# One iteration of a pipelined attention-and-feed-forward kernel, laid out anew on VectorE, ScalarE, GpSimd and SyncE

## Chip, cores and metric

The kernel runs on one core of a Trainium2 chip. The metric is device time in microseconds (us) of one execution, as the median of several runs. PE is TensorE (PEld its weight loads), DVE is VectorE, ACT is ScalarE, POOL is GpSimd, and SP is SyncE, which here only issues DMAs.

## What is computed

One transformer layer on x of shape (8, 1024, 512), float32, with 16 heads of 32:

```python
Q, K, V = (split_heads(x @ W.T + b) for W, b in ((Wq, bq), (Wk, bk), (Wv, bv)))
scores = jnp.einsum('bhid,bhjd->bhij', Q, K) / jnp.sqrt(jnp.float32(hd))
scores = jnp.where(causal_mask, -jnp.inf, scores) + decay      # decay = -(i - j)
out = jnp.einsum('bhij,bhjd->bhid', jax.nn.softmax(scores, axis=-1), V)
attn = merge_heads(out) @ Wo.T + bo
...
xh = x @ H                                    # Hadamard, 512 x 512
xq = quantize(xh)                             # 4 bits, one scale a row
ffn = jnp.einsum('bsi,oi->bso', xq, ternary(weight))
...
x = x + layernorm(attn(layernorm(x)))
x = x + layernorm(ffn(layernorm(x)))
```

## The kernel before, in words

Only `fast_path` runs for these inputs (a flag computed on the chip would otherwise start `general_path`). The 8192 rows are worked in 32 steps of 256 rows (two tiles of 128), four steps a batch element. Each of the five engines has a program of its own, written out by hand; the engines meet at semaphores alone, and each executes its own list strictly in the order in which it is written. So the order of the calls in `fast_path` is the schedule.

The main loop is `for s in range(STEPS - 1)`, written once for each engine. Iteration s holds work of several steps at once, with n = s + 1, m = s + 2 and k = s - 1:

- step m, front: statistics of x (`front_stats`, DVE), their columns (`front_columns`, POOL), the normalised x (`front_norm`, ACT) and its split into two f16 halves (`front_high`, ACT; `front_low`, DVE), turned by DMA (`turn_x`, SP);
- step n: query and key products (`qk`, PE, groups 0 to 3), kept as a high half (`qk_high_part`, ACT) and a low half (`qk_low_part`, DVE), copied by 12 DMAs into the operand of the scores (`restack`, SP), squares (`square_of`, POOL) and norms (`keep_norms`, DVE), values (`values`, PE; `keep_v`, ACT; `mix_values`, three DMAs on SP), the scores for the row maxima (`scores`, PE, 0 to 3; `maxima` and `split_max`, DVE);
- step s: `turn_max` (PE) and `keep_max` (ACT), `max_rows` (two DMAs), the keys' products (`keys`, PE, four groups of two halves), `exps` (ACT), `clear_future` (POOL, the causal mask, two instructions a group), `weigh` (PE), the reciprocal (`invert`, ACT, a logarithm and an exponential), `normalise` (DVE, three instructions), and the two halves of the result (`heads_high`, ACT; `heads_low`, POOL);
- step k: the output product (`out_product`, PE, tiles 0 and 1), `y_out` and `y_stats` (DVE), `y_columns` (POOL), the residual (`residual`, DVE), the first two levels of the Hadamard transform (`fold`, `fold_again`, DVE), its split (`x2_high`, ACT; `x2_low`, DVE) and turning (`turn_x2`, SP);
- step k - 1, feed-forward: `transform` (PE), `find_scale` (DVE), `square_sum`, `round_levels`, `level` (ACT), `turn_q` (PE), `keep_q` (ACT), `second` (PE), `scale_out` and `z_stats` (DVE), `z_columns` (POOL), `norm_z` (ACT), `finish_out` (POOL, two additions and the DMA of the output).

PSUM: the score tiles and the head outputs have two banks each, and all other products share four, `ps_job`. `ORDER` gives the twenty products of an iteration to these four in turn, and `claim` makes PE wait until the product that held the bank four places earlier has been read. Three of these waits matter below. `values(n, 1)` takes the bank of the second feed-forward product, so PE waits there for `scale_out(k - 1, 1)` on DVE (L1107). `scores(n, 2)` and `scores(n, 3)` wait for `maxima(n, 0)` and `maxima(n, 1)` (L1010). `qk(n, 0)` of the next iteration waits for `keep_norms` (L1002).

Other waits across engines that the prediction speaks of: `out_product(k, 0)` on PE waits for all four `heads_low(k, .)` on POOL; `weigh(s, 3)` waits for `normalise(s, 1)`; `load_res(k)` on SP waits for `finish_out(k - 2)`; `scores(n, 0)` waits for all twelve DMAs of `restack`; and in the first iterations for `load_rows`, the constant rows of the scores' operand.

Lines of the profile: L1316 is every split product (`qk`, `values`, `out_product`), L996 `qk_low_part`, L658 `qk_high_part`, L1032/1034/1037 `normalise`, L1049 `y_out`, L1065 `residual`, L1071/1072 `fold`, L1080/1081 `fold_again`, L1086 `x2_low`, L1107 `scale_out`, L1010 `maxima`, L1002 `keep_norms`, L1017/1019/1022 `split_max`, L514 `clear_future`, L520 `heads_low`, L535/538 `finish_out`, L691/693 `invert`, L376 `restack`, L318 `load_front`, L1417 `keys`.

## Time and profile before

| | |
|---|---|
| time, median of 3 runs | 1220.31 us (1218.34 to 1220.6) |
| the profiled execution | 1217.23 us, span 1215.2 us |
| PE | busy 1106.2 us (91%) |
| DVE | busy 972.1 us (80%) |
| ACT | busy 745.7 us (61%) |
| POOL | busy 661.7 us (54%) |
| DMA queues | 54.7% and 4.7% of 16 engines' span |
| TensorE clock granted | 0.973 in the mean, 1.00 in the middle |
| chain that ended last | DVE 48%, ACT 19%, issue 17%, PE 10% |

Busy time is the union of the instructions' spans on an engine. Matmuls overlap one another in the pipeline, so a busy PE is not the same as a PE that streams all the time; start to start tells that better. "Issue" in the chain is time in which an engine waited for nothing that the profile shows. The first 33 us or so are weights and first products, and from about 1120 us on the last step drains; in between the loop runs with a period of some 35 us.

### The profile page before, as it was taken

Reading aid. Unit: us, or ns where it says so; the run is one execution under the profiler, and the core shown is the slowest. Engines: PE = TensorE matmul, PEld = TensorE weight load, DVE = VectorE, ACT = ScalarE, POOL = GpSimd, SP = SyncE. Lnnn points to the kernel's source line nnn. Section 1 sums busy time; section 2 is a strip of 40 time slices with the busy share of each in tenths; the row PEclk is TensorE's granted clock in tenths of the full one; section 3 lists DMA queues with packets and bytes.
Section 4 is the critical chain, followed back from the end, with each engine's and each line's share of the span. In section 5 each row is a group of like instructions: output and inputs, shape, how many; then the busy total and the mean of one; then the engine's idle time right before and its main releaser. Section 6 shows DMA issues by size and latency. Waiting matters only on the chain.

```text
span 1215.2 us, 45316 instructions
## 1 busy us (share of the span) xinstructions
PE 1106.2 (91%) x18656; PEld 727.5 (60%) x18656; DVE 972.1 (80%) x2082; ACT 745.7 (61%) x1622; POOL 661.7 (54%) x1101
## 2 busy tenths in 40 slices
PE   5899999999999999999999999999999999999551
PEld 3566656666666666666666666666666666666320
DVE  6658998888888888889888888888888889887662
ACT  5445567666566666655667666666766655666441
POOL 2334565565555556555555566565556565565442
PEclk9999999999999999999999999999999999999865
DMA  9746665675667566566665666666666655654231
GB/s 271 175 106 134 120 134 138 151 145 136 128 127 146 134 137 158 129 136 140 126 133 136 155 143 134 128 126 136 146 140 150 136 133 138 130 114 104 69 70 37
DMA packets 204692, 161.85 MB, mean 133 GB/s; under 512 B 150432, under 2 KB 150688, under 8 KB 204384
## 3 DMA queue, kind: packets, MB, share of 16 engines
q1 hardware_dynamic: 199600, 141.34, 54.7%
q0 software_dynamic: 4880, 17.57, 4.7%
q8 instruction: 148, 2.42, 0.9%
q14 instruction: 64, 0.52, 0.2%
HBM read 40.87 MB, written 16.78 MB: 47 GB/s over the span
## 4 chain that ended last, share of the span: by engine, by line
DVE 48%; ACT 19%; issue 17%; PE 10%; DMA 1%; SPq 1%; POOL 1%; POOLq 0%; ACTq 0%; DVEq 0%
PE f_job L1316 7%; DVE f_rmax L1010 5%; DVE f_inverse L1034 4%; DVE f_x2l L1086 4%; DVE f_o L1032 4%; ACT f_stage L658 4%; ACT f_PT L680 3%; DVE f_z L1107 3%; DVE f_y L1072 3%; DVE f_stage L996 3%; ACT f_unread L709 3%; DVE f_fst L968 3%; DVE f_bst L1042 2%; DVE f_o L1037 2%; DVE f_folded_x L1081 2%
## 5 line engine op out<-in xcount | busy, mean ns | idle before, releaser
L514 POOL TENSOR_SCALAR_AFFINE_SELECT f_PT<-f_PT 64x512 f32<-64x512 f32 (+1 forms) x256 | 186.2, 746 | 89.4 <-ACT f_PT L680 58.2
L529 POOL TENSOR_TENSOR f_square<-f_stage 128x512 bf16<-128x512 f16 x128 | 130.3, 1038 | 137.1 <-ACT f_stage L658 125.1
L996 DVE SCALAR_TENSOR_TENSOR f_stage<-f_job,f_bias,f_stage 128x256 f16<-128x256 f32 x256 | 111.2, 476 | 71.8 <-ACT f_stage L658 71.7
L1316 PE MATMUL f_job<-f_xTh,f_wqh 128*128 128x256 f16 x512 | 140.9, 275 | 15.6 <-DVE f_wkl L869 14.3
L698 ACT ACTIVATE f_OTh<-f_o 128x256 f16<-128x256 f32 x128 | 52.2, 408 | 158.4 <-DVE f_o L1037 158.4
L1316 PE MATMUL f_job<-f_xTh,f_wql 128*128 128x256 f16 x512 | 140.1, 274 | 0.0
L1316 PE MATMUL f_job<-f_xTl,f_wqh 128*128 128x256 f16 x512 | 140.1, 274 | 0.0
L1316 PE MATMUL f_job<-f_xTh,f_wkh 128*128 128x256 f16 x512 | 139.7, 273 | 0.0
L1316 PE MATMUL f_job<-f_xTh,f_wkl 128*128 128x256 f16 x512 | 139.7, 273 | 0.0
L1316 PE MATMUL f_job<-f_xTl,f_wkh 128*128 128x256 f16 x512 | 139.6, 273 | 0.0
L1316 PE MATMUL f_job<-f_wvh,f_xTh 128*128 128x512 f16 x256 | 97.8, 382 | 28.7 <-DVE f_z L1107 28.7
L658 ACT ACTIVATE f_stage<-f_job,f_bias 128x256 f16<-128x256 f32 x256 | 105.7, 464 | 20.8 <-PE f_job L1316 14.1
L520 POOL TENSOR_TENSOR f_OTl<-f_o,f_OTh 128x256 f16<-128x256 f32 x128 | 85.1, 665 | 59.7 <-ACT f_OTh L698 59.7
L680 ACT ACTIVATE f_PT<-f_st 128x512 f32<-128x512 f32 x192 | 105.7, 590 | 6.9 <-PE f_st L1417 6.9
L1417 PEld LDWEIGHTS f_st<-f_stacks 128*64 128x64 f16 x2432 | 68.1, 110 | 52.4 <-issue 32.4
L1316 PE MATMUL f_job<-f_woh,f_OTh 128*128 128x512 f16 x256 | 98.6, 385 | 0.4 <-POOL f_OTl L520 0.4
L666 ACT ACTIVATE f_V<-f_job 128x512 f32<-128x512 f32 x64 | 38.1, 597 | 98.9 <-PE f_job L1316 98.9
L1316 PE MATMUL f_job<-f_woh,f_OTl 128*128 128x512 f16 x256 | 97.9, 382 | 0.0
L1316 PE MATMUL f_job<-f_wol,f_OTh 128*128 128x512 f16 x256 | 97.7, 382 | 0.0
L1316 PE MATMUL f_job<-f_wvh,f_xTl 128*128 128x512 f16 x256 | 97.5, 381 | 0.0
L1316 PE MATMUL f_job<-f_wvl,f_xTh 128*128 128x512 f16 x256 | 97.3, 380 | 0.0
L1417 PE MATMUL f_st<-f_stacks 128*64 128x128 f16 (+1 forms) x2432 | 91.8, 214 | 3.9 <-ACT f_PT L684 3.9
(189 smaller groups left out, 3049.8 us busy)
## 6 DMA issues: line engine op xcount, KB each, us to landing
f_stacks<-f_stage SPq DMA_DIRECT2D x380, 128.0 KB
f_xin<-x SPq DMA_DIRECT2D x32, 512.0 KB, 4.6
f_x<-x SPq DMA_DIRECT2D x32, 512.0 KB, 3.9
out<-f_z POOLq DMA_DIRECT2D x32, 512.0 KB, 4.2
f_Vmix<-f_V SPq DMA_DIRECT2D x32, 256.0 KB
f_Vmix<-f_V SPq DMA_DIRECT2D x64, 128.0 KB
f_stacks<-rows_const SPq DMA_DIRECT2D x3, 512.0 KB, 7.1
f_stacks<-wqT SPq DMA_DIRECT2D x2, 512.0 KB, 5.0
```

The source lines that it names most:

```text
L514: nc.gpsimd.affine_select(out=d, in_=d, compare_op=ALU.is_ge, fill=0.0, base=odd * SUB, pattern=[[0, 4], [0, TP], [1, SUB]], channel_multi ...
L520: nc.gpsimd.tensor_tensor(OT[s % 2][1][:, g, :], o32[:, g % 2, :], OT[s % 2][0][:, g, :], ALU.subtract).then_inc(OTl_made, 1)
L529: nc.gpsimd.tensor_tensor(square[:, 2 * m + pair, :], h, h, ALU.mult).then_inc(squared, 1)
L658: nc.scalar.activation(stage[:, 2 * m, g, :], bank("qk", g)[:, m * W2:(m + 1) * W2], ACT.Identity, bias=bias[:, m, g:g + 1]).then_inc(qk_h ...
L680: nc.scalar.activation(dst, src, ACT.Exp, scale=1.0 / SS).then_inc(expd, 1)
L698: nc.scalar.activation(OT[s % 2][0][:, g, :], o32[:, g % 2, :], ACT.Copy).then_inc(OTh_made, 1)
L996: nc.vector.scalar_tensor_tensor(stage[:, 2 * m + 1, g, :], bank("qk", g)[:, m * W2:(m + 1) * W2], bias[:, m, g:g + 1], stage[:, 2 * m, g, ...
L1010: nc.vector.tensor_reduce(rmax[:, n % 2, SLOTS * i:SLOTS * i + SLOTS], score_bank(n, i)[:, 0:SLOTS * BW].rearrange("q (i k) -> q i k", k=B ...
L1032: nc.vector.tensor_tensor(heads, heads, inverse[:, g % 2, :], ALU.mult).then_inc(o_scaled, 1)
L1034: nc.vector.tensor_tensor(inverse[:, g % 2, :], ps_o[g % 2][:, W2:D], inverse[:, g % 2, :], ALU.mult).then_inc(o_error, 1)
L1316: mm = pe.matmul(dst, lhs[a](c), rhs[b](c), start=(n == 0), stop=(n == 3 * KC - 1))
L1417: mm = pe.matmul(ps_st[half][upper * SUB:(upper + 1) * SUB, i * W2 + q * SUB:i * W2 + (q + w) * SUB], Ks[js % 3][:, h, c * SUB:(c + 1) * SUB],
```

## The change

In the loops of DVE, ACT, POOL and SP, calls stand in another order, and some have moved to the next or the previous iteration. PE's program and every operation are as they were. Written out in the difference below; in short:

- SP: `mix_values` of a step is issued one iteration later, after `load_front` and before `restack`; `load_rows` comes after `restack`.
- POOL: `heads_low(k, 3)` stands first, `square_of(n, 1)` after two `clear_future`; `front_columns` works a step ahead and stands between `heads_low(s, 1)` and `heads_low(s, 2)`; `finish_out` is last, behind `heads_low(s, 2)`.
- ACT: `invert(s, 2)`, `heads_high(s, 1)` and `heads_high(s, 2)` have moved into the next iteration, behind `qk_high_part(n, 0)`; `keep_max` stands ahead of `qk_high_part(n, 1)`, both `front_norm` earlier, `level(k - 1, 0)` between the two first `exps`.
- DVE: `front_stats` works a step ahead and stands at the end; both `qk_low_part(n, 2)` and `(n, 3)` stand ahead of `find_scale(k - 1, 1)`; `front_low` ahead of both `y_out`; `scale_out(k - 1, 0)` ahead of `residual`; `scale_out(k - 1, 1)` ahead of `fold_again(k, 1)`; `maxima` are spread out; `normalise(s, 1)` is between the last two.

```diff
@@ -425,19 +425,21 @@
                     load_res(k)
                 if has(m + 1):
                     load_front(m + 1)
-                if s < 2:
-                    load_rows(n)
+                if s:
+                    mix_values(s)
                 restack(n, 0)
                 restack(n, 1)
                 restack(n, 2)
+                if s < 2:
+                    load_rows(n)
                 if has(m):
                     turn_x(m)
-                mix_values(n)
                 if has(k):
                     turn_x2(k, 0)
                     turn_x2(k, 1)
 
             last = STEPS - 1
+            mix_values(last)
             max_rows(last)
             load_res(last - 1)
             turn_x2(last - 1, 0)
@@ -544,18 +546,17 @@
             pool.wait_ge(qk_low, 8)
             for r in range(4):
                 pool.dma_start(*stack_piece(0, 2, r)).then_inc(first_stacked, 16)
+            front_columns(2)
             for s in range(STEPS - 1):
                 n, m, k = s + 1, s + 2, s - 1
-                square_of(n, 0)
                 if has(k):
                     heads_low(k, 3)
-                if has(m):
-                    front_columns(m)
-                if has(n):
-                    square_of(n, 1)
+                square_of(n, 0)
                 if has(s):
                     clear_future(s, 0)
                     clear_future(s, 1)
+                if has(n):
+                    square_of(n, 1)
                 if has(k):
                     y_columns(k)
                 if has(s):
@@ -566,10 +567,12 @@
                     clear_future(s, 3)
                     heads_low(s, 0)
                     heads_low(s, 1)
+                if has(m + 1):
+                    front_columns(m + 1)
+                if has(s):
+                    heads_low(s, 2)
                 if has(k - 1):
                     finish_out(k - 1)
-                if has(s):
-                    heads_low(s, 2)
 
             last = STEPS - 1
             heads_low(last - 1, 3)
@@ -756,41 +759,48 @@
             for s in range(STEPS - 1):
                 n, m, k = s + 1, s + 2, s - 1
                 qk_high_part(n, 0)
+                if s:
+                    invert(k, 2)
                 if has(k):
                     invert(k, 3)
+                if s:
+                    heads_high(k, 1)
+                    heads_high(k, 2)
+                keep_max(s)
                 qk_high_part(n, 1)
-                keep_max(s)
+                if has(m):
+                    front_norm(m, 0)
+                qk_high_part(n, 2)
                 if has(k):
                     heads_high(k, 3)
-                qk_high_part(n, 2)
                 if has(k - 1):
                     square_sum(k - 1, 0)
                     round_levels(k - 1, 0)
+                qk_high_part(n, 3)
                 if has(m):
-                    front_norm(m, 0)
-                qk_high_part(n, 3)
+                    front_norm(m, 1)
+                exps(s, 0, 0)
+                if s == 0:
+                    keep_ffscale()
                 if has(k - 1):
                     level(k - 1, 0)
-                exps(s, 0, 0)
                 exps(s, 0, 1)
-                if s == 0:
-                    keep_ffscale()
-                    keep_tern()
                 if has(m):
-                    front_norm(m, 1)
                     front_high(m)
                 exps(s, 1, 0)
                 exps(s, 1, 1)
+                if s == 0:
+                    keep_tern()
                 if has(k - 1):
                     square_sum(k - 1, 1)
                     round_levels(k - 1, 1)
                     level(k - 1, 1)
                     keep_q(k - 1, 0)
                 invert(s, 0)
-                exps(s, 2, 0)
                 invert(s, 1)
                 if has(k - 1):
                     keep_q(k - 1, 1)
+                exps(s, 2, 0)
                 exps(s, 2, 1)
                 keep_v(n, 0)
                 if has(k):
@@ -802,11 +812,11 @@
                 keep_v(n, 1)
                 if has(k - 1):
                     norm_z(k - 1)
-                invert(s, 2)
-                heads_high(s, 1)
-                heads_high(s, 2)
 
             last = STEPS - 1
+            invert(last - 1, 2)
+            heads_high(last - 1, 1)
+            heads_high(last - 1, 2)
             keep_max(last)
             invert(last - 1, 3)
             heads_high(last - 1, 3)
@@ -1140,56 +1150,56 @@
             maxima(0, 2)
             maxima(0, 3)
             split_max(0)
+            front_stats(2)
             for s in range(STEPS - 1):
                 n, m, k = s + 1, s + 2, s - 1
                 qk_low_part(n, 0)
                 if has(k):
                     normalise(k, 3)
                 qk_low_part(n, 1)
-                if s == 0:
-                    keep_norms(0)
-                if has(m):
-                    front_stats(m)
                 if has(k - 1):
                     find_scale(k - 1, 0)
                 qk_low_part(n, 2)
+                if s == 0:
+                    keep_norms(0)
+                qk_low_part(n, 3)
+                if s < 4:
+                    weight_guard(s)
                 if has(k - 1):
                     find_scale(k - 1, 1)
-                qk_low_part(n, 3)
                 if s == 0:
                     fold_bias()
-                if has(k):
-                    y_out(k, 0)
-                if s < 4:
-                    weight_guard(s)
                 if has(m):
                     front_low(m)
                 if has(k):
+                    y_out(k, 0)
                     y_out(k, 1)
                     y_stats(k)
                 normalise(s, 0)
-                if has(k):
-                    residual(k)
                 if has(k - 1):
                     scale_out(k - 1, 0)
                 if has(k):
+                    residual(k)
                     fold(k, 0)
+                    fold(k, 1)
                     fold_again(k, 0)
-                    fold(k, 1)
-                    fold_again(k, 1)
                 if has(k - 1):
                     scale_out(k - 1, 1)
+                maxima(n, 0)
+                if has(k - 1):
                     z_stats(k - 1)
                 if has(k):
+                    fold_again(k, 1)
                     x2_low(k, 0)
-                normalise(s, 1)
-                maxima(n, 0)
                 maxima(n, 1)
                 keep_norms(n)
                 if has(k):
                     x2_low(k, 1)
                 maxima(n, 2)
+                normalise(s, 1)
                 maxima(n, 3)
+                if has(m + 1):
+                    front_stats(m + 1)
                 split_max(n)
                 normalise(s, 2)
```

On VectorE, in the part of an iteration that begins with `residual` (f_x11 is the residual input of step k, f_job3 and f_job1 the banks of the two feed-forward products, f_job2 that of the first scores). Before:

```order
L1065 SCALAR_TENSOR_TENSOR f_x11<-f_y,f_small,f_x11 128x512 x2
L1107 TENSOR_TENSOR f_z<-f_job3,f_ffscale_bc 128x512
L1071 TENSOR_TENSOR f_y<-f_x11 128x256
L1072 TENSOR_TENSOR f_y<-f_x11 128x256
L1080 TENSOR_TENSOR f_folded_x<-f_y 128x2x128
L1081 TENSOR_TENSOR f_folded_x<-f_y 128x2x128
L1071 TENSOR_TENSOR f_y<-f_x11 128x256
L1072 TENSOR_TENSOR f_y<-f_x11 128x256
L1080 TENSOR_TENSOR f_folded_x<-f_y 128x2x128
L1081 TENSOR_TENSOR f_folded_x<-f_y 128x2x128
L1107 TENSOR_TENSOR f_z<-f_job1,f_ffscale_bc 128x512
L1042 BN_STATS f_bst<-f_z 128x6 x2
```

And with the change, from the same place (line numbers there are higher by 10):

```order
L1117 TENSOR_TENSOR f_z<-f_job3,f_ffscale_bc 128x512
L1075 SCALAR_TENSOR_TENSOR f_x11<-f_y,f_small,f_x11 128x512 x2
L1081 TENSOR_TENSOR f_y<-f_x11 128x256
L1082 TENSOR_TENSOR f_y<-f_x11 128x256
L1081 TENSOR_TENSOR f_y<-f_x11 128x256
L1082 TENSOR_TENSOR f_y<-f_x11 128x256
L1090 TENSOR_TENSOR f_folded_x<-f_y 128x2x128
L1091 TENSOR_TENSOR f_folded_x<-f_y 128x2x128
L1117 TENSOR_TENSOR f_z<-f_job1,f_ffscale_bc 128x512
L1020 TENSOR_REDUCE f_rmax<-f_job2 128x8
L1052 BN_STATS f_bst<-f_z 128x6 x2
```

The first `scale_out` has gone ahead of the residual, the second ahead of one `fold_again`, and the first of the `maxima` follows at once.

On GpSimd, around the end of an iteration (f_OTh1 and f_OTl1 are the halves of the heads' results of one step, f_z the output rows). Before:

```order
L514 AFFINE_SELECT f_PT1<-f_PT1 128x8x64
L520 TENSOR_TENSOR f_OTl1<-f_o32,f_OTh1 128x256 [waits f_OTh_made] x2
L535 TENSOR_TENSOR f_z<-f_z,f_x11 128x512 [waits f_z_normed] x2
L538 DMA out<-f_z 128x2x512 [waits f_out_made]
L520 TENSOR_TENSOR f_OTl1<-f_o32,f_OTh1 128x256 [waits f_OTh_made]
L529 TENSOR_TENSOR f_square<-f_stage 128x512 [waits f_norms_product,f_qk_high]
L529 TENSOR_TENSOR f_square<-f_stage 128x512
L520 TENSOR_TENSOR f_OTl1<-f_o32,f_OTh1 128x256 [waits f_OTh_made]
```

And with the change (line numbers higher by 2):

```order
L516 AFFINE_SELECT f_PT1<-f_PT1 128x8x64
L522 TENSOR_TENSOR f_OTl1<-f_o32,f_OTh1 128x256 [waits f_OTh_made] x2
L468 TENSOR_SCALAR f_small<-f_f_mv 128x2 [waits f_xn_made,f_f_stats_made]
L469 TENSOR_SCALAR f_small<-f_f_mv 128x2
L471 TENSOR_TENSOR f_small<-f_small,f_minus_half 128x2 [waits f_f_veps_made]
L474 TENSOR_TENSOR f_small<-f_small 128x2 [waits f_f_rstd_made,f_f_turned_sign]
L522 TENSOR_TENSOR f_OTl1<-f_o32,f_OTh1 128x256 [waits f_OTh_made]
L537 TENSOR_TENSOR f_z<-f_z,f_x11 128x512 [waits f_z_normed] x2
L540 DMA out<-f_z 128x2x512 [waits f_out_made]
L522 TENSOR_TENSOR f_OTl1<-f_o32,f_OTh1 128x256 [waits f_OTh_made]
L531 TENSOR_TENSOR f_square<-f_stage 128x512 [waits f_norms_product,f_qk_high]
```

The two additions and the output's DMA have moved from ahead of the third `heads_low` of a step to directly ahead of its fourth, and the four small `front_columns` instructions stand ahead of the third.

## Rows read from the trace of the kernel before

**Rows 1.** Busy time by engine in four iterations (busy us, instructions, clock, DMA share, GB/s):

```profile
602.40:743.20 140.80, 136.12 (x2334) 90.28 (x2332) 118.28 (x254) 91.19 (x200) 81.71 (x137) 1.00 0.63 137
```

**Rows 2.** Waits in 461 to 1024 us, sixteen iterations (total us, times, longest):

```profile
PEld f_job L1316 <- DVE f_z L1107: 20.5, 16, 1.6
...
PEld f_job L1390 <- DVE f_rmax L1010: 6.0, 12, 0.7
PEld f_job L1316 <- DVE f_nmax L1002: 3.5, 16, 0.3
...
PEld f_job L1316 <- DVE f_stage L996: 1.9, 11, 0.2
```

**Rows 3.** Timeline of PE and its weight loads (start, us, instruction, [idle before <- releaser]):

```profile
633.43 0.28 PE L1316 MATMUL f_job<-f_xTh,f_wqh 128*128 128x256 f16 x1
...
647.10 0.39 PE L1316 MATMUL f_job<-f_woh,f_OTh 128*128 128x512 f16 x1
...
663.39 0.39 PE L1316 MATMUL f_job<-f_wvh,f_xTh 128*128 128x512 f16 x1 [1.01 <-DVE f_z L1107]
...
667.36 0.09 PEld L1390 LDWEIGHTS f_job<-f_stacks 107*32 107x32 f16 x1 [0.67 <-DVE f_rmax L1010]
668.49 0.10 PEld L1316 LDWEIGHTS f_job<-f_xTh,f_wqh 128*128 128x128 f16 x1 [0.21 <-DVE f_nmax L1002]
```

**Rows 4.** Timeline of DVE, from the second `y_out` to `scale_out` of that iteration:

```profile
653.41 0.69 DVE L1049 SCALAR_TENSOR_TENSOR f_y<-f_job,f_bo_bc 128x512 f32<-128x512 f32 x1 [0.40 <-PE f_job L1316]
...
656.05 0.43 DVE L1032 TENSOR_TENSOR f_o<-f_o,f_inverse 128x256 f32<-128x256 f32 x1 [0.34 <-ACT f_inverse L693]
...
657.31 1.41 DVE L1065 SCALAR_TENSOR_TENSOR f_x<-f_y,f_small,f_x 128x512 f32<-128x512 f32 x2
658.64 0.68 DVE L1107 TENSOR_TENSOR f_z<-f_job,f_ffscale_bc 128x512 f32<-128x512 f32 x1
...
659.57 0.88 DVE L1072 TENSOR_TENSOR f_y<-f_x 128x256 f32<-128x256 f32 x1
...
661.98 0.43 DVE L1080 TENSOR_TENSOR f_folded_x<-f_y 128x256 f32<-128x256 f32 x1
...
662.65 0.69 DVE L1107 TENSOR_TENSOR f_z<-f_job,f_ffscale_bc 128x512 f32<-128x512 f32 x1
```

**Rows 5.** Timeline of POOL: `clear_future` of two groups of that iteration:

```profile
650.49 1.30 POOL L514 TENSOR_SCALAR_AFFINE_SELECT f_PT<-f_PT 64x512 f32<-64x512 f32 x2
...
658.26 1.91 POOL L514 TENSOR_SCALAR_AFFINE_SELECT f_PT<-f_PT 64x512 f32<-64x512 f32 x2 [0.94 <-ACT f_PT L680]
```

**Rows 6.** Timeline of POOL: `finish_out` and the fourth `heads_low`, around 633.43:

```profile
635.09 2.50 POOL L535 TENSOR_TENSOR f_z<-f_z,f_x 128x512 f32<-128x512 f32 x2
637.88 0.82 POOL L538 DMA_DIRECT2D out<-f_z  x1 [0.30 <-POOL f_z L535]
...
643.59 0.67 POOL L520 TENSOR_TENSOR f_OTl<-f_o,f_OTh 128x256 f16<-128x256 f32 x1
644.59 0.23 POOL L466 TENSOR_SCALAR f_small<-f_f_mv 128x2 f32<-128x2 f32 x1 [0.32 <-DVE f_f_mv L971]
...
645.96 0.20 POOL L472 TENSOR_TENSOR f_small<-f_small 128x2 f32<-128x2 f32 x1
```

**Rows 7.** Timeline of ACT: `qk_high_part(n, 0)` and, behind `invert(k, 3)`, `qk_high_part(n, 1)`:

```profile
639.25 0.82 ACT L658 ACTIVATE f_stage<-f_job,f_bias 128x256 f16<-128x256 f32 x2
...
640.70 0.82 ACT L658 ACTIVATE f_stage<-f_job,f_bias 128x256 f16<-128x256 f32 x2
```

**Rows 8.** Timeline of SP's queue: last load, then `restack`:

```profile
644.02 0.46 SPq L318 DMA_DIRECT2D f_xin<-x  x1
648.44 9.89 SPq L376 DMA_DIRECT2D f_stacks<-f_stage  x12
```

**Rows 9.** Head: PE's wait in iteration 0 (timeline), and landing of the constant rows (issues):

```profile
57.50 0.41 PE L1417 MATMUL f_st<-f_stacks 128*64 128x128 f16 x8 [3.90 <-ACT f_PT L684]
...
f_stacks<-rows_const SPq DMA_DIRECT2D x3, 512.0 KB, 7.1
```

## The prediction

> **What bounds the kernel now.** I read the busy time by engine over four whole iterations first [rows 1]: PE is busy 136.1 of 140.8 us, DVE 118.3, ACT 91.2, POOL 81.7, at the full clock. So PE's stream is what everything else must keep up with, and a new order elsewhere can win only what PE still waits. The list of waits says how much that is [rows 2]: in sixteen iterations PE's weight loads waited 20.5 us for DVE's `scale_out` (L1107), 6.0 for `maxima` (L1010), 3.5 for `keep_norms` (L1002) and 1.9 for `qk_low_part` (L996): 1.28, 0.38, 0.22 and 0.12 us an iteration, 2.0 together. PE's timeline shows where [rows 3]. One iteration starts at 633.43 and the next at 668.49, a period of 35.06 us. The wait for `scale_out` stands ahead of `values(n, 1)` at 663.39, the other two behind it, at 667.36 and 668.49. I count in T, us from 633.43.
>
> DVE's timeline [rows 4] shows the chain behind the large wait. The second `y_out` starts when PE has made its product (653.41, T + 19.98). From there DVE works almost without a pause: `y_stats`, `normalise(s, 0)`, residual, `scale_out` 0, two folds, two `fold_again`, `scale_out` 1, which ends at 662.65 + 0.69 = 663.34. That is 9.93 us, and PE goes on 0.05 us behind it.
>
> **The change, part by part.**
>
> *The chain on DVE.* Out of it goes one `fold_again` (661.98 to 662.65, 0.67 us [rows 4]), which now follows the second `scale_out`. With both folds ahead of `fold_again`, two short waits for the instruction just before fall away, an estimated 0.1 each. `normalise(s, 0)` waited 0.34 us for ACT; now both `invert` come before `exps(s, 2, .)`, and I take 0.4 off. But `scale_out` 0 has moved ahead of the residual and there has to wait for PE's first feed-forward product, an estimated 0.3. So far -0.67 - 0.2 - 0.4 + 0.3 = -1.0.
>
> Against this stands a collision. Two instructions of `clear_future` take 1.30 us alone, but 1.91 when they start at 658.26 beside the residual and the folds [rows 5]. In the same stretch the fold at 659.57 took 0.88 us, where a fold_again of the same size took 0.43 [rows 4]: it ended with, not beside, POOL's second instruction. DVE paid some 0.46 us, because one of the two ran under `scale_out` 0, which reads PSUM. With the change `scale_out` 0 is over by then. The inverts ahead of `exps(s, 2, .)` keep `clear_future(s, 2)` near T + 24.7, and the residual, at about T + 24.4, is followed by 2 us of folds, all with both operands in SBUF like the fold that was held. The price lies between nothing (if the residual isn't held and POOL is done before the folds) and 1.30; I take 1.2, near the upper end, as both instructions now meet such operations. It was 0.46, so +0.74. The chain is then 0.25 us shorter.
>
> The residual itself was never seen stretched. The Trainium skill (SBUF — State Buffer, Who interferes with whom) says that a DVE instruction with two SBUF inputs contends with a GpSimd instruction that reads SBUF, and that the loser blocks for the whole instruction; the stretched fold agrees with it, at 0.88 us. By that rule the residual is held too; were it only the folds, the collision would cost 0 to 0.6 and the chain would be some 0.6 to 1.2 us shorter still.
>
> *The smaller waits.* `qk_low_part(n, 1)` no longer comes late: `keep_max` and `front_norm` don't stand before its partner for long, and DVE reaches it about T + 9, a little ahead of PE: -0.12. `maxima(n, 0)` follows `scale_out` 1 at once, where it stood behind `z_stats`, `x2_low` and a `normalise`: PE finds its bank free at `scores(n, 2)`. The weight load waited 0.67 at 667.36, but part of that is the end of PE's own work before it; I take 0.3. `keep_norms` comes in good time: -0.22. The sum for an iteration is 0.12 + 0.25 + 0.3 + 0.22 = 0.9 us.
>
> *The end of the loop on DVE and ACT.* `normalise(s, 1)` now lies behind `z_stats`, `fold_again`, both `x2_low`, three `maxima` and `keep_norms`, and `weigh(s, 3)` waits for it. From the start of `scale_out` 1 these are, by DVE's starts elsewhere, about 7.5 us; PE gets to `weigh` 8.0 us after that start (0.75 to the values, 668.49 - 663.39 = 5.10 less the two waits of 0.55 to the next iteration [rows 3], an estimated 2.7 of `qk`). This costs nothing, with some 0.3 us of cover. ACT takes `invert(k, 2)` only behind `qk_high_part(n, 0)`. `qk_high_part` and `invert` take 1.45 us together [rows 7], so the inverse is there about T + 4.3, where `normalise(k, 2)` started before (behind `split_max`, about T + 4). Nothing, with the pause that follows as cover.
>
> *POOL.* `out_product(k, 0)` started at 647.10, T + 13.7 [rows 3], and needs the fourth `heads_low`, which ran from 643.59 to 644.26, 2.8 us ahead [rows 6]. Now that waits behind more. ACT reaches `heads_high(k, 1)` and `(k, 2)` about T + 5.0 to 6.0, the small front columns take 1.6 us (644.59 to 646.16), a `heads_low` 0.67, `finish_out` 2.50 + 0.30 + 0.82 = 3.6 [rows 6]. From T + 5.4: 0.7 + 1.6 + 0.7 + 3.6 + 0.7 ends at T + 12.7. PE wants it at T + 13.5. I cost it at nothing, but the cover has shrunk from 2.8 to 0.8 us.
>
> *SP.* `load_res(k)` waits for the additions of `finish_out`, now done near T + 11 (before, T + 4.2). Then two loads (0.6 and 0.5) and the three DMAs of `mix_values` (an estimated 1.8) must be issued ahead of `restack`, which began at 648.44, T + 15.0, after a pause from 644.48 [rows 8]. 11.0 + 2.9 = 13.9 fits into that pause. `restack` then lands no later than before, though behind the loads' and `mix_values`' traffic. `scores(n, 0)` may even be late by 0.9 us, as long as PE waits behind it for `scale_out` anyway. Nothing.
>
> *Head and tail.* In iteration 0 PE waited 3.90 us for `exps`, which stood behind `keep_tern` [rows 9]; they change places, and I take 2.3 off. `front_stats(2)` now stands ahead of the low parts, +1.5. `load_rows` is issued behind twelve DMAs and took 7.1 us to land [rows 9]: in iterations 0 and 1 the scores may wait, +2 in all. Tail: as before, an estimated -0.5. Together +0.7, between -4 and +5.
>
> *The sum.* The feed-forward terms are there in 29 of the 31 iterations: 29 x 0.9 = 26.1. 1217.2 - 26.1 + 0.7 = 1191.8 for the profiled execution, which lies 3.1 us under the median of the runs shown. So 1195 us as a median.
>
> **The rivals.**
>
> *A, the collision doesn't happen.* Then 0.7 to 1.2 us more leave the chain and the wait of 1.28 goes nearly whole: up to 0.12 + 1.28 + 0.3 + 0.22 = 1.9 us an iteration, 55 us, down to about 1165. For it: the residual's own spans were never stretched. Against it: POOL's 1.91 us beside it, which began under the residual. Chance 0.17.
>
> *B, the collision takes all.* If also `x2_low` or `front_low` are held, or DVE comes late to `normalise(s, 0)`, 0.6 to 0.9 us go back and 0 to 0.3 remain: 1210 to 1221. For it: ACT's work ahead of `invert(s, 0)` is much the same, and in the operations that read SBUF twice DVE meets POOL in other places too. Chance 0.12.
>
> *C, POOL becomes the bound (slower).* It decides at `heads_low(k, 3)`: each us by which it ends after T + 13.5 is a us for PE. It takes 0.8 us to get there and 1.7 to cancel the gain. Each of `finish_out`'s additions, which read SBUF twice, can be held, and a late `finish_out` holds `load_res`, `mix_values` and `restack` as well. At 2.2 us late PE waits 1.4, a loss of 0.5 net, 29 x 0.5 = 15, plus the head: 1236. Against it: DVE reads mostly PSUM at T + 8 to 12. Chance 0.11.
>
> That the change doesn't do what it says can be left out: order and waits are plain in the lists.
>
> **How the numbers follow.** The forecast has 0.60, spread 1185 to 1206 by the head's bounds and 0.3 us an iteration; A 0.17, B 0.12, C 0.11. I predict 1195 us, the likeliest case. The range reaches into A to 1172 and takes in B to 1219. A measurement tells 0.2% (2.4 us) from no change. Faster by more than that: the forecast, A and half of B, 0.83; the same 0.06; slower 0.11.
>
> **What would show it.** Right: period 34.1 to 34.3 us; PE's wait for `scale_out` still there, at 0.7 to 1.2 us; the waits for `maxima` and `keep_norms` gone; the residual's instructions (0.74 us each so far) stretched beside POOL's mask, the folds not; `split_max` short, as `finish_out` no longer lies beside it; the fourth `heads_low` ending 0.5 to 1 us ahead of `out_product`. Wrong: a wait of PE for `heads_low` or for the DMAs of `restack`, which would make it C; no wait for `scale_out` at all, which would make it A; a head longer by over 5 us.

## The result, and the profile after

| | before | after |
|---|---|---|
| median, 20 runs each | 1219.55 us | 1225.21 us |
| smallest to largest | 1216.19 to 1222.8 | 1218.21 to 1230.04 |
| ratio | | 1.0041, 95% interval 1.0027 to 1.0055 |
| profiled execution, span | 1217.23, 1215.2 us | 1226.29, 1224.3 us |

The changed kernel is slower by 0.4%. The prediction was 1195 us, in a range that ended at 1219. Ratios here and below are of fast runs alone, which matters in experiment 5 only, where two of eight runs lie more than 1.5% above the fastest.

Of the page of the changed kernel, the busy times and the chain that ended last, by engine and by line:

```profile
PE 1106.3 (90%) x18656; PEld 738.7 (60%) x18656; DVE 916.8 (75%) x2082; ACT 753.6 (62%) x1622; POOL 670.0 (55%) x1101
...
PE 23%; DMA 19%; issue 15%; POOL 15%; DVE 14%; SPq 11%; ACT 3%; POOLq 0%; ACTq 0%; DVEq 0%
DMA f_Vmix<-f_V 13%; PE f_job L1326 10%; SPq L376 5%; POOL f_z L537 5%; POOL f_OTl L522 4%; DVE f_x L1075 4%; PE f_o L1444 3%; POOL f_PT L516 3%; DVE f_bst L1052 3%; PE f_o L1449 3%; PE f_job L1489 2%; DMA f_stacks<-f_stage 2%; DVE f_y L1082 2%; DVE f_folded_x L1091 2%; PE f_st L1427 1%
```

DVE, 48% of the chain before, is down to 14%. Its place has gone to a path that was not there before: `finish_out` on POOL (L537), SyncE's issues (SPq), and the copies of `mix_values` (`DMA f_Vmix<-f_V`).

PE's waits in the window of [rows 2], about sixteen iterations (total us, times, longest; these are of the matmuls, where [rows 2] has the weight loads):

```profile
PE f_o L1444 <- DMA f_Vmix<-f_V: 14.1, 14, 2.7
PE f_job L1400 <- DMA f_stacks<-f_stage: 3.6, 5, 1.1
PE f_job L1326 <- DVE f_z L1117: 3.4, 9, 0.5
PE f_job L1402 <- DMA f_stacks<-f_stage: 1.6, 2, 1.2
```

The waits for `maxima` and `keep_norms` are gone, as predicted. That for `scale_out` is small: on the weight loads, to compare with the 20.5 us of [rows 2], it is 6.9 us, 0.43 an iteration, where 0.7 to 1.2 was the sign of being right. In their place `weigh(s, 0)` (L1444) waits for `mix_values`, and the scores (L1400, L1402) sometimes wait for `restack`.

I take the iteration with the longest wait. T is 674.08 in it: its transposed maxima (`turn_max`) start at 680.87, and T lies 6.79 before that, as in the iteration of [rows 3] (its own first product starts at 674.49). SyncE's queue in it (start, us, line):

```profile
681.42 1.20 SPq L393 DMA_DIRECT2D f_stacks<-f_mrow  x2
685.26 0.40 SPq L358 DMA_DIRECT2D f_x<-x  x1
685.71 0.47 SPq L318 DMA_DIRECT2D f_xin<-x  x1
686.27 0.54 SPq L383 DMA_DIRECT2D f_Vmix<-f_V  x1
686.86 0.76 SPq L384 DMA_DIRECT2D f_Vmix<-f_V  x1
687.66 1.46 SPq L385 DMA_DIRECT2D f_Vmix<-f_V  x1
689.22 9.55 SPq L376 DMA_DIRECT2D f_stacks<-f_stage  x12
```

POOL in front of it:

```profile
682.75 2.49 POOL L537 TENSOR_TENSOR f_z<-f_z,f_x 128x512 f32<-128x512 f32 x2
685.53 0.82 POOL L540 DMA_DIRECT2D out<-f_z  x1 [0.30 <-POOL f_z L537]
686.39 0.68 POOL L522 TENSOR_TENSOR f_OTl<-f_o,f_OTh 128x256 f16<-128x256 f32 x1
```

And on PE the `weigh` that waits:

```profile
697.04 0.32 PE L1444 MATMUL f_o<-f_PT,f_Vmix 128*32 128x64 f32 x8 [2.66 <-DMA f_Vmix<-f_V]
```

`load_res` is issued at 685.26, T + 11.2, right behind `finish_out`; the three copies are issued from T + 12.2 to T + 15.0. These are about the times that the prediction had (11.0 and 13.9). But then they have to land, and that takes long, as the page's row of issues says (KB each, median us from the start of the issue to landing):

```profile
f_Vmix<-f_V SPq DMA_DIRECT2D x32, 256.0 KB, 7.2
f_Vmix<-f_V SPq DMA_DIRECT2D x64, 128.0 KB, 7.2
```

In this iteration the third copy took longer, as the chain that ended last shows (start, us, what):

```profile
687.66 9.24 DMA f_Vmix<-f_V
```

Its issue starts at T + 13.6, and it has landed at 687.66 + 9.24 = 696.90, T + 22.8. PE was ready for `weigh(s, 0)` at 697.04 - 2.66 = 694.38, T + 20.3, and went on at T + 23.0. That is the worst case of the loop. In the median of iterations 2 to 29 the third copy's issue starts at T + 13.4 and it has landed at T + 20.6, 0.3 us after PE is ready; the waits run from nothing to 2.66 us, 23.3 us in all.

### The profile page after: what moved, and what is told of

Its sections match the earlier page's. It is cut to its first block, busy times and chain, and to the rows that moved or that the text cites. A ratio compares the mean times of both kernels' runs of the same rounds, so it can differ in the third digit from the quotient of the medians.

```text
span 1224.3 us, 45316 instructions
## 1 busy us (share of the span) xinstructions
PE 1106.3 (90%) x18656; PEld 738.7 (60%) x18656; DVE 916.8 (75%) x2082; ACT 753.6 (62%) x1622; POOL 670.0 (55%) x1101
## 4 chain that ended last, share of the span: by engine, by line
PE 23%; DMA 19%; issue 15%; POOL 15%; DVE 14%; SPq 11%; ACT 3%; POOLq 0%; ACTq 0%; DVEq 0%
DMA f_Vmix<-f_V 13%; PE f_job L1326 10%; SPq L376 5%; POOL f_z L537 5%; POOL f_OTl L522 4%; DVE f_x L1075 4%; PE f_o L1444 3%; POOL f_PT L516 3%; DVE f_bst L1052 3%; PE f_o L1449 3%; PE f_job L1489 2%; DMA f_stacks<-f_stage 2%; DVE f_y L1082 2%; DVE f_folded_x L1091 2%; PE f_st L1427 1%
## 5 line engine op out<-in xcount | busy, mean ns | idle before, releaser
L516 POOL TENSOR_SCALAR_AFFINE_SELECT f_PT<-f_PT 64x512 f32<-64x512 f32 (+1 forms) x256 | 195.2, 781 | 181.2 <-ACT f_PT L683 124.3
L1326 PE MATMUL f_job<-f_xTh,f_wqh 128*128 128x256 f16 x512 | 140.8, 275 | 17.0 <-DMA f_xTl<-f_xl 14.5
L707 ACT ACTIVATE f_x2h<-f_folded_x 128x512 f16<-128x512 f32 x64 | 40.3, 630 | 138.0 <-DVE f_folded_x L1091 138.0
L1444 PE MATMUL f_o<-f_PT,f_Vmix 128*32 128x64 f32 (+1 forms) x2048 | 72.9, 226 | 33.0 <-DMA f_Vmix<-f_V 23.3
```

Of the source, the lines that this page charges most:

```text
L516: nc.gpsimd.affine_select(out=d, in_=d, compare_op=ALU.is_ge, fill=0.0, base=odd * SUB, pattern=[[0, 4], [0, TP], [1, SUB]], channel_multi ...
L1326: mm = pe.matmul(dst, lhs[a](c), rhs[b](c), start=(n == 0), stop=(n == 3 * KC - 1))
L1444: pe.matmul(dst[rows, c * SUB:(c + 1) * SUB], v[:, g * P + r * HD:g * P + (r + 1) * HD], weights[keys, r, c * SUB:(c + 1) * SUB], start=Tr ...
```

## The experiments

Times are medians. Beside experiments 1 to 4 the kernel before was at 1221.11 us, beside 5 to 7 at 1219.0. A period is the time from the start of one `turn_max` to the next; every fourth is longer than the others in all kernels.

**1. Only `mix_values` back at its old place.**

```diff
-                if s:
-                    mix_values(s)
                 restack(n, 0)
...
                     turn_x(m)
+                mix_values(n)
...
-            mix_values(last)
             max_rows(last)
```

> The changed kernel with one part undone: mix_values(n) again at the end of SyncE's iteration, behind turn_x(m), everything else as changed. Theory S (the copies of mix_values are the loss: they are issued behind load_res, which waits for finish_out, land 7.2 us later beside two loads and the output, and the first weigh of the iteration waits up to 2.7 us for them): the waits of PE for f_Vmix go (14.1 us in sixteen iterations, 0.9 an iteration), the period comes to 34.1 to 34.3 us as in the one iteration of the changed kernel that was not held, and the time to 1195 to 1203 us. Rival P (the new order of GpSimd and VectorE is worth little, and something else would be late in the same place): 1215 to 1226 us, period 34.8 to 35.1.

Measured: 1189.58 us, ratio 0.9739 (0.9718 to 0.9761). In the same window as above, PE's waits:

```profile
PE f_job L1324 <- DVE f_z L1115: 6.0, 15, 0.5
PE f_job L1400 <- issue: 0.6, 1, 0.6
```

Four iterations' busy time, of the changed kernel and then of this one (order as in [rows 1]):

```profile
602.40:743.20 140.80, 134.84 (x2325) 91.19 (x2323) 109.84 (x249) 92.43 (x200) 83.03 (x136) 0.99 0.67 137
```

```profile
602.40:743.20 140.80, 139.22 (x2417) 93.38 (x2415) 114.01 (x257) 96.58 (x210) 87.49 (x142) 1.00 0.72 148
```

PE does 2417 instead of 2325 matmuls in the same 140.8 us. The period is 33.47 us, in every fourth iteration 35.15; the mean is 33.89, against 35.11 before. Sixteen iterations took 561.8 us before, 563.1 with the change and 542.9 here. So the one moved call costs some 20 us in sixteen iterations, and 36 us in all. The copies now land in this time:

```profile
f_Vmix<-f_V SPq DMA_DIRECT2D x32, 256.0 KB, 3.2
f_Vmix<-f_V SPq DMA_DIRECT2D x64, 128.0 KB, 3.3
```

Theory S holds, and the rival, that the rest of the change is worth little, falls. The gain is larger than expected, though: the time lies below the 1195 to 1203 us, and the period below the 34.1 to 34.3.

**2. `mix_values` one call earlier, ahead of `load_res`.**

```diff
                 max_rows(s)
+                if s:
+                    mix_values(s)
                 if has(k):
                     load_res(k)
                 if has(m + 1):
                     load_front(m + 1)
-                if s:
-                    mix_values(s)
...
-            mix_values(last)
             max_rows(last)
+            mix_values(last)
```

> The changed kernel with mix_values(s) one step earlier: right behind max_rows(s) and ahead of load_res(k), and the same at the end, behind max_rows(last). The copies then don't wait for finish_out and go out near T + 8 to 9, 3 to 4 us sooner. Theory S: that is enough for weigh at T + 20, the waits for f_Vmix go, 1195 to 1205 us. Rival D (the copies' traffic itself is the trouble, as it falls together with restack's in this half of the iteration wherever it stands): PE waits for f_stacks or f_Vmix as before, 1213 to 1226 us.

Measured: 1191.05 us, ratio 0.9763 (0.9737 to 0.9789). That is again faster than expected (1195 to 1205). In the sixteen iterations no wait for f_Vmix or f_stacks is left, and the copies land in 3.2 to 3.3 us, at T + 12.9. The copies may stand in this part of the iteration, and beside `restack`; what costs the time is their place behind the wait for `finish_out`. Rival D falls.

**3. The kernel before, with only `mix_values` moved.**

```diff
                     load_front(m + 1)
+                if s:
+                    mix_values(s)
                 if s < 2:
                     load_rows(n)
...
-                mix_values(n)
                 if has(k):
...
+            mix_values(last)
             max_rows(last)
```

> The kernel before with one part of the change: mix_values(s) issued behind the two loads and ahead of restack, in the next iteration; GpSimd, VectorE and ScalarE as before. finish_out is done near T + 4 here, so the loads and copies go out early, near T + 11, behind the wait for the row maxima. Theory S in its strict form (the place in SyncE's order is enough): weigh waits for f_Vmix here too, some 0.5 to 1 us an iteration, 1232 to 1250 us. Rival L (it takes the late finish_out as well, that is, both parts together): the copies land in time, within 3 us of the kernel before, 1217 to 1223 us.

Measured: 1224.93 us, ratio 1.0028 (1.0015 to 1.0041). SyncE's queue in an iteration whose T is 601.31:

```profile
611.26 0.58 SPq L358 DMA_DIRECT2D f_x<-x  x1
...
612.45 0.53 SPq L383 DMA_DIRECT2D f_Vmix<-f_V  x1
...
613.66 0.91 SPq L385 DMA_DIRECT2D f_Vmix<-f_V  x1
```

Here `load_res` has nothing to wait for, and the copies are out by T + 13.3. They take 6.0 to 6.2 us to land in the median. The third has mostly landed at T + 18.8, some 1.7 us before PE wants it, and only two iterations of sixteen wait, 0.8 us together, with periods as before (35.06). The strict form of theory S falls; rival L, that it takes the late `finish_out` too, holds for the loop, though the time is 2 us over its 1217 to 1223. The loss of 4 us (7.0 between the two profiled executions) lies outside the steady loop. The third `turn_max` comes at 116.1 us (112.0 before), and from the last `turn_max` to the end of the span it is 90.0 us (86.5 before). In the tail PE waits 4.0 us for `max_rows(last)`, which is queued behind `mix_values(last)`. The changed kernel has that wait too:

```profile
PE f_st L1427 <- DMA f_stacks<-f_mrow: 4.3, 1, 4.3
```

The order of these two calls isn't the whole cause, since in experiment 2, with `max_rows(last)` ahead, it is still 3.1 us, and 0.2 in experiment 1, where the copies went out an iteration earlier.

**4. The changed kernel, with `finish_out` earlier on POOL.**

```diff
                     heads_low(s, 1)
+                if has(k - 1):
+                    finish_out(k - 1)
                 if has(m + 1):
                     front_columns(m + 1)
                 if has(s):
                     heads_low(s, 2)
-                if has(k - 1):
-                    finish_out(k - 1)
```

> The changed kernel with finish_out(k - 1) moved ahead of front_columns(m + 1) and heads_low(s, 2) on GpSimd; SyncE as changed. load_res and the copies behind it can be issued some 3 us sooner. Theory S: part of the loss goes, 1200 to 1215 us, unless heads_low(s, 2) is now late for out_product. Rival D or P: 1220 to 1230 us.

Measured: 1227.23 us, ratio 1.0049 (1.0032 to 1.0066). The number is that of rival P, but not for its reason:

```profile
PE f_job L1326 <- POOL f_OTl L522: 11.6, 16, 0.9
PE f_job L1326 <- DVE f_z L1117: 6.4, 16, 0.5
PE f_job L1479 <- ACT f_q L723: 6.3, 16, 0.4
```

The copies are issued from T + 10.1 instead of T + 12.2, still land in 7.2 to 7.3 us, and no wait for them is left. So issue time plus landing against T + 20.3 decides. But `heads_low` has become the wait, in all sixteen iterations. POOL in one of them, whose T is 604.62:

```profile
616.37 0.67 POOL L522 TENSOR_TENSOR f_OTl<-f_o,f_OTh 128x256 f16<-128x256 f32 x1
618.37 0.67 POOL L522 TENSOR_TENSOR f_OTl<-f_o,f_OTh 128x256 f16<-128x256 f32 x1 [1.33 <-ACT f_OTh L701]
```

The fourth ends at T + 14.4 instead of T + 13.0, and PE, which wants it at T + 13.5, waits 0.85. That is the wait that rival C named, but not by its path: POOL is free at 617.04 and stands idle 1.33 us for ACT's `heads_high(k, 3)`. ACT in the same iteration shows why:

```profile
616.44 0.82 ACT L642 ACTIVATE f_xin<-f_xin,f_small 128x512 f32<-128x512 f32 x1 [3.78 <-POOL f_small L474]
...
617.88 0.41 ACT L701 ACTIVATE f_OTh<-f_o 128x256 f16<-128x256 f32 x1
```

`front_norm(m, 0)` (L642) waits 3.78 us for `front_columns` on POOL, which now come behind the 3.6 us of `finish_out`, and `heads_high(k, 3)` (L701) stands behind it in ACT's list. Without ACT's delay the fourth `heads_low` would have ended near T + 13.1, in time. So neither of these two places of `finish_out` is harmless: late, it holds SyncE, early, it holds ACT and through it PE. A third place, between `front_columns` and `heads_low(s, 2)`, would let ACT go on and let SyncE go sooner than in the changed kernel by one `heads_low`, 0.67 us; no run shows it.

**5. `mix_values` between the two loads.**

```diff
+                if s:
+                    mix_values(s)
                 if has(m + 1):
                     load_front(m + 1)
-                if s:
-                    mix_values(s)
```

> The changed kernel with mix_values(s) between load_res(k) and load_front(m + 1), so still behind the wait for finish_out. It separates two parts of theory S: the late issue (T + 12.2 to 14.2) and the 1 MB of loads and output ahead of the copies (landing 7.2 us, against 3.2 where the copies stand alone). If the traffic ahead counts, the copies go out 0.5 us sooner and land some 1.5 us faster, PE's waits for them (0.9 us an iteration) go, and the time is 1190 to 1200. If the landing stays near 7 us, only 0.5 us of the wait goes and the time is 1208 to 1220.

Measured: 1224.38 us over all eight runs, 1211.85 to 1234.05; the six that the ratio counts, up to 1229.56, have a median of 1220.3. The ratio is 1.0023 (0.9988 to 1.0058), so no change is shown. The profiled execution took 1216.43 us, less than the median. Neither expectation came true as a whole. The copies do land sooner, in 5.3 to 5.6 us, and no wait for them is left. The waits have moved on to `restack`:

```profile
PE f_job L1400 <- DMA f_stacks<-f_stage: 16.1, 12, 2.5
PE f_job L1402 <- DMA f_stacks<-f_stage: 8.8, 4, 2.5
```

Together 24.9 us, more than the waits for f_Vmix and f_stacks in the changed kernel (19.3). The end of `finish_out` lets go the output, one load, the copies and the other load, 2 MB, with `restack`'s 1.5 MB behind them. Which of the two that PE reads comes late depends on the order; in this order it is the later one. The start of `restack` counts too: the third copy's issue takes some 2.3 us here, and the first DMA of `restack` starts at T + 16.0 in the median, against 14.3 in the changed kernel. But in experiment 3 it starts at T + 15.4, and PE, which reads at the same T + 27.8 to 27.9, waits for it hardly at all (0.6 us in sixteen iterations). Half a us of later start does not make 1.6 us of wait an iteration, so what is let go ahead of it must count for part. What isn't settled is whether `load_front`'s 512 KB ahead of `restack` are needed for that. No run shows the order that would tell, `load_front` behind `restack`.

**6. The head: `load_rows` back, then `front_stats(2)` too.** Both on top of experiment 1.

```diff
+                if s < 2:
+                    load_rows(n)
                 restack(n, 0)
                 restack(n, 1)
                 restack(n, 2)
-                if s < 2:
-                    load_rows(n)
```

> The changed kernel with mix_values(n) at its old place (as the first experiment) and load_rows(n) of iterations 0 and 1 issued ahead of restack again. In the first experiment's trace PE waited 6.7 us, in two waits, for the rows of load_rows. If these waits are the whole price of that move, they go and the time falls from 1189.6 us to 1183 to 1186. Rival: the scores wait there for restack's own transfers just as long, and no more than 1 us is won, 1188 to 1190.

Measured: 1184.15 us, ratio 0.9724 (0.9707 to 0.9741). The waits for the constant rows (6.7 us in experiment 1) are gone, and 5.4 us with them. The kernel before was 2.1 us faster beside this run than beside experiment 1, so of the 5.4 perhaps only 3.3 are this move's; in the profiled executions the third `turn_max` comes 5.6 us sooner. This is the fastest of the kernels here, 2.8% under the kernel before.

```diff
             split_max(0)
-            front_stats(2)
...
                 qk_low_part(n, 1)
+                if s == 0:
+                    front_stats(2)
```

(and `front_columns(2)` on POOL likewise, behind `square_of(1, 0)`.)

> As the run before, and in addition front_stats(2) with its small columns back inside iteration 0, behind the second low part. I put the move of front_stats(2) at 1.5 us in the prediction; the first transposed maxima came 1.5 us later in the first experiment too (45.36 against 43.85 us). If that carries through to the end, 1.5 us less than the run before; rival: a later wait in iteration 0 or 1 takes it back, and the two runs are within 0.5 us.

Measured: 1186.32 us (1185.38 to 1186.87), against 1182.47 to 1188.26 for the run before: a difference of 2 us the other way, within the spread of the two. The first `turn_max` is 0.6 us sooner (44.95 against 45.51) and the next period 0.2 us longer. The 1.5 us that I had put down for this move are not there.

**7. One term of DVE's chain undone.** On top of experiment 1.

```diff
                     fold_again(k, 0)
+                    fold_again(k, 1)
                 if has(k - 1):
                     scale_out(k - 1, 1)
...
-                    fold_again(k, 1)
                     x2_low(k, 0)
```

> The first experiment with one DVE term undone: fold_again(k, 1) ahead of scale_out(k - 1, 1) again. It is the term of 0.67 us by which the prediction shortened the chain in front of values(n, 1). PE still waits 0.38 us for scale_out, so the chain is the bound and all of it should come back: 29 x 0.67 = 19 us, 1189.6 + 19 = 1209 us, with PE's wait near 1.05. Rival: the chain has slack elsewhere (the wait is partly PE's own pipeline), and less than half returns, under 1199.

Measured: 1208.66 us, ratio 0.9926 (0.9907 to 0.9945), 19.1 us more than experiment 1, where 19 was expected. That it fits to 0.1 us is luck: against the kernel before, 2.1 us faster beside this run, it is 21 us, and the sixteen iterations are 12.3 us longer (555.2 against 542.9), 0.77 each, not 0.67. The wait for `scale_out` in the sixteen iterations:

```profile
PE f_job L1324 <- DVE f_z L1115: 16.4, 16, 1.1
```

1.03 us an iteration against 0.38. DVE's chain is the bound once the copies are out of the way, and a term of it counts in full. The other terms (`maxima`, `keep_norms`, the order of the folds) were not undone one by one.

## Why the prediction was wrong

**The step that failed is SP, costed at "Nothing".** Its times of issue were right: `load_res` near T + 11.0 (measured 11.2), the last copy's issue ending at T + 13.9 (14.2 in the median, 15.0 in the iteration shown), `restack` starting at T + 14.3 in the median and so no later than before. But the step ended with the issue and asked only whether `restack` came in time. It never asked when the moved transfers themselves had to be there, and who read them. `weigh(s, 0)` does, at T + 20.3. Before the change `mix_values` was issued an iteration earlier and no wait of PE named it, so neither a wait nor a landing time stood in my rows. The rows had a bound, though: `load_rows` took 7.1 us to land behind twelve DMAs [rows 9]. By the prediction's own times the third copy's issue starts near T + 13.3 (three in 1.8 us, ending at 13.9), and 13.3 + 7.1 = T + 20.4: no cover at all against T + 20.3. Measured is a landing 7.2 us behind the start in the median and up to 9.2. A wait of 0 to 2.7 us followed, the one that experiments 1 and 2 take away. `restack`, which the step did ask about, came late as well, but less: 5.2 us in the sixteen iterations against 14.1.

Rival C came near. It named the path (a late `finish_out` "holds load_res, mix_values and restack as well"), but it measured the danger at `heads_low`, and gave everything slower a chance of 0.11. For the copies T + 11, the time of the forecast itself, was late enough. In the changed kernel `heads_low` was no wait of PE's, as costed: in the iteration shown the fourth ends at 686.39 + 0.68 = T + 13.0, for a predicted T + 12.7. Experiment 4 shows what happens when the fourth comes 1.4 us later.

**The rest held in kind, not in all sizes.** Experiment 1 is the change without that step. Its chain on DVE, in the iteration that answers to [rows 4]:

```profile
641.27 0.69 DVE L1057 SCALAR_TENSOR_TENSOR f_y<-f_job,f_bo_bc 128x512 f32<-128x512 f32 x1 [1.13 <-PE f_job L1324]
...
643.54 0.43 DVE L1040 TENSOR_TENSOR f_o<-f_o,f_inverse 128x256 f32<-128x256 f32 x1
...
645.07 0.69 DVE L1115 TENSOR_TENSOR f_z<-f_job,f_ffscale_bc 128x512 f32<-128x512 f32 x1 [0.19 <-PE f_job L1487]
645.68 1.82 DVE L1073 SCALAR_TENSOR_TENSOR f_x<-f_y,f_small,f_x 128x512 f32<-128x512 f32 x2
647.42 0.87 DVE L1079 TENSOR_TENSOR f_y<-f_x 128x256 f32<-128x256 f32 x1
648.22 0.41 DVE L1080 TENSOR_TENSOR f_y<-f_x 128x256 f32<-128x256 f32 x1
...
649.89 0.68 DVE L1115 TENSOR_TENSOR f_z<-f_job,f_ffscale_bc 128x512 f32<-128x512 f32 x1
```

with POOL's mask beside it:

```profile
645.91 2.11 POOL L514 TENSOR_SCALAR_AFFINE_SELECT f_PT<-f_PT 64x512 f32<-64x512 f32 x2 [0.70 <-ACT f_PT L681]
```

- The whole chain, from the second `y_out` to the end of `scale_out` 1, is 649.89 + 0.68 - 641.27 = 9.30 us, against 9.93: 0.63 shorter, where 0.25 was predicted. The wait for `invert` went (0.34, for 0.4); `scale_out` 0 waits 0.19 (for 0.3).
- The collision was mis-sized, at +0.74. The residual is stretched from 1.41 to 1.82, and one fold to 0.87; a fold had 0.88 before too. That makes +0.41. The other folds have their 0.41. The prediction's sign, the residual stretched and the folds not, is half right. The Trainium skill (SBUF — State Buffer, Who interferes with whom) says that a DVE instruction with two SBUF inputs contends with a GpSimd instruction that reads SBUF. The residual, never seen stretched before, now is, and so the trace agrees. The price of the residual came on top of the fold's, which stayed. POOL lost as much: its two mask instructions took 2.11 us, for 1.30 alone. Each of the four instructions held (the second of the residual, the fold, both of the mask) lost 0.40 to 0.46 us, when 0.5 to 0.6 us of the other engine's instruction was left. No run puts the residual ahead of `scale_out` 0 again, to show whether the price goes.
- From the start of `values(n, 1)` to the next iteration it is 655.17 - 650.63 = 4.54 us, for 5.10 before: 0.56 less, where `maxima` and `keep_norms` were put at 0.52.
- The mean period fell by 1.22 us, where 0.9 was predicted; 0.63 and 0.56 make up 1.19 of it. The difference is about that of the collision, 0.41 for 0.74. The wait for `scale_out` that is left is 10.5 us on the weight loads, 0.66 an iteration, just under the 0.7 to 1.2 of the sign.
- The cover of `normalise(s, 1)` was added up wrongly, 8.0 - 7.5 is 0.5 and not 0.3 us; no wait of PE for it appears in the loop, so nothing hung on it.
- Head and tail were put at +0.7. The third `turn_max` comes at 119.3 us in experiment 1 and at 112.0 before, a loss of 7.3, of which `load_rows` is 5.6 (put at 2): with it at its old place the third comes at 113.8. From the last `turn_max` to the end it is 88.6 us (86.5 before), where -0.5 was predicted, and 90.6 in the changed kernel. `keep_tern` behind `exps` brought 2.8, put at 2.3: PE's wait there is 1.1 us instead of 3.90 [rows 9].

In sum, 1215.2 - 29 x 1.22 + 7.3 + 2.1 = 1189.2 us, and the span of experiment 1 is 1188.8. The forecast of 1195 us for the whole change would have been 5 us too high for it. That it comes so near is partly luck: a larger gain in the loop (29 x 0.32 = 9 us) and a costlier head and tail (9 us) nearly cancel, and most of the 5 us are the 3.1 added to get from the profiled execution to the median. The 36 us between this and the changed kernel are the one step.

## What to carry to other kernels

When a DMA is moved to a later place in a queue, add three things and not one: when the queue gets to it (behind the waits of everything ahead of it), how long it takes to land there beside the traffic that is let go with it (the longest case too, not the median alone), and when its reader wants it. A transfer that no wait names in the profile of before has its slack unseen, not unlimited, so look up the reader in the code. And a wait of one queue entry is a wait of all entries behind it: two moves that are each harmless in the loop, `mix_values` behind `load_res` (experiment 3) and `finish_out` to a later place (experiment 1), together cost 36 us here. The same holds of a list on an engine: in experiment 4 one wait on ACT held everything behind it.

## What the runs showed of the hardware

The same three copies landed, in the median and from the start of the issue, in 3.2 to 3.3 us with no load just ahead of them (experiments 1 and 2), in 5.3 to 5.6 with the output's DMA and one load issued just before (experiment 5), in 6.0 to 6.2 with two loads (experiment 3) and in 7.2 to 7.3 with the output and both loads (the changed kernel and experiment 4). The changed kernel and experiments 2 and 5 differ only in the place of these copies in SyncE's order. Single copies spread widely: 3.2 to 9.2 us in the changed kernel, 2.5 to 6.1 in experiment 1.

A pause of PE can cost more than its length. Windows of the changed kernel around the wait of 2.66 us (window, length, then PE, PEld, DVE, ACT, POOL busy, granted clock, DMA share, GB/s):

```profile
694.00:697.00 3.00, 0.38 (x11) 0.24 (x10) 2.23 (x5) 0.77 (x2) 2.03 (x5) 1.00 1.06 212
697.00:698.00 1.00, 0.96 (x45) 0.87 (x49) 0.00 (x0) 0.00 (x0) 0.86 (x2) 1.00 1.05 195
698.00:699.00 1.00, 1.00 (x40) 0.88 (x36) 0.00 (x0) 0.78 (x2) 0.01 (x1) 0.54 1.10 211
699.00:700.00 1.00, 1.00 (x16) 0.31 (x10) 0.89 (x3) 0.21 (x2) 0.00 (x0) 0.50 1.12 236
...
701.00:702.00 1.00, 1.00 (x5) 0.41 (x4) 0.00 (x0) 1.00 (x3) 0.00 (x0) 0.75 2.01 133
702.00:703.00 1.00, 1.00 (x6) 0.43 (x5) 0.86 (x2) 0.48 (x1) 0.45 (x1) 1.00 0.27 47
```

After nearly 3 us in which PE was idle but for 0.38, and about 1 us after it had gone on, the granted clock fell from 1.00 to 0.50, that is from 2.4 to 1.2 GHz, and stayed there until about 701.5. The period of this iteration is 37.62 us, 4.15 more than the 33.47 of experiment 1. The wait alone explains 2.66. The other 1.5 us are about what 3.5 us at half the clock lose, an estimated 1.7; that they are due to the clock is worked out, not shown by a run of its own. Not every pause did this. The clock fell likewise after waits of 1.84 us (at 341.63) and 1.38 us (at 767.78) for f_Vmix, but after one of 2.02 us (at 521.62) it stayed at 1.00.
